# Reordering scaling, transposes and reads inside the states of a selective scan

## The reference, cut to what matters

```python
xi, z = jnp.split(xn @ in_proj, 2, axis=-1)          # 512 channels each
xi = silu(causal_conv4(xi) + conv_b)
dt, Bm, Cm = jnp.split(xi @ x_proj, [16, 32], axis=-1)
delta = softplus(dt @ dt_w + dt_b)
A = -exp(A_log)                                      # 512 channels x 16 states
h = exp(delta * A) * h + (delta * xi) * B            # over the tokens, for each state
y = sum over states of h * C
y = (y + xi * D) * silu(z)
out = x + y @ out_proj
```

## Time and profile before

| | |
|---|---|
| median of 3 runs | 575.18 us (573.67 to 576.09) |
| profiled execution | 575.25 us, of which the traced span is 573.5 us |
| busy: PE, DVE, POOL, ACT | 486.3, 462.5, 387.0, 371.7 us |
| mean granted PE clock | 0.93 of full |

### The profile page before, as it was taken

The page is one execution under the profiler, slowest core; times in us unless marked ns, Lnnn a source line. Parts: engine busy times, 40 slices in busy tenths (PEclk is TensorE's granted clock), DMA queues, the critical chain, the costliest instruction groups (busy, mean ns, idle before and its releaser), DMA issues.

```text
span 573.5 us, 7946 instructions
## 1 busy us (share of the span) xinstructions
PE 486.3 (85%) x2777; PEld 340.7 (59%) x2777; DVE 462.5 (81%) x531; ACT 371.7 (65%) x650; POOL 387.0 (67%) x235
## 2 busy tenths in 40 slices
PE   8968999879868999998689999896797758789992
PEld 6424765455557675655575666465786546678651
DVE  4779989968899888879997888699989989951512
ACT  3766677667875766698858676888558759821210
POOL 5049978756798877759986777589959979510001
PEclk9978999955989999979999999799999979999997
DMA  9331111110111111111111111101211391039004
GB/s 290 107 113 37 38 37 38 39 39 37 34 40 38 37 39 38 39 37 38 38 38 38 38 37 38 39 2 37 75 37 38 110 405 45 2 87 345 0 1 151
DMA packets 17919, 38.88 MB, mean 68 GB/s; under 512 B 1665, under 2 KB 10497, under 8 KB 17874
## 3 DMA queue, kind: packets, MB, share of 16 engines
q1 hardware_dynamic: 17874, 38.32, 19.6%
HBM read 36.08 MB, written 2.23 MB: 67 GB/s over the span
## 4 chain that ended last, share of the span: by engine, by line
PE 47%; DVE 26%; issue 12%; ACT 10%; POOL 2%; DVEq 0%; ACTq 0%; POOLq 0%
DVE scanmem L1724 16%; PE hT L837 9%; PE pp L542 6%; PE pp L566 6%; PE yacc L600 4%; DVE yTd L1744 4%; PE pp L629 4%; PE pp L592 2%; ACT dA L1257 2%; PE dA L802 2%; POOL scanmem L1399 2%; PE pp L578 2%; ACT hc L1267 2%; PE pp L701 1%; PE pp L773 1%
## 5 line engine op out<-in xcount | busy, mean ns | idle before, releaser
L1399 POOL TENSOR_TENSOR scanmem<-par,scanmem 128x1024 f32<-128x1024 f32 x128 | 300.4, 2366 | 87.9 <-ACT carry L1282 41.6
L1257 ACT ACTIVATE dA<-par,Aneg 128x512 f32<-128x512 f32 x256 | 171.1, 690 | 45.2 <-DVE scanmem L1724 43.3
L837 PE MATMUL hT<-con,scanmem 128*128 128x128 f32 x1024 | 153.1, 290 | 43.2 <-DVE yTd L1744 21.3
L837 PEld LDWEIGHTS hT<-con,scanmem 128*128 128x128 f32 x1024 | 121.4, 148 | 100.0 <-issue 35.3
L1724 DVE TENSOR_TENSOR_SCAN scanmem<-dA,scanmem 128x512 f32<-128x512 f32 x128 | 150.3, 1207 | 22.3 <-ACT dA L1257 21.7
L1724 DVE TENSOR_TENSOR_SCAN scanmem<-dA,carry,scanmem 128x512 f32<-128x512 f32 x128 | 157.1, 1267 | 11.8 <-ACT dA L1257 11.5
L1267 ACT ACTIVATE hc<-hT,CTs 128x512 f32<-128x512 f32 x128 | 87.4, 683 | 75.4 <-PE hT L837 75.1
L600 PE MATMUL yacc<-con,hc 128*128 128x128 f32 x512 | 78.8, 294 | 11.2 <-ACT hc L1267 10.9
L600 PEld LDWEIGHTS yacc<-con,hc 128*128 128x128 f32 x512 | 62.9, 151 | 17.6 <-ACT hc L1267 13.7
L1744 DVE SCALAR_TENSOR_TENSOR yTd<-hT,CTs,yTd 128x512 f32<-128x512 f32 x85 | 62.1, 730 | 12.4 <-PE hT L837 12.0
L542 PE MATMUL pp<-xnT,wi 128*128 128x512 f32 x120 | 61.2, 640 | 4.9 <-ACT xnT L1036 3.2
(11 more groups left out here) (195 smaller groups left out, 507.6 us busy)
## 6 DMA issues: line engine op xcount, KB each, us to landing
scanmem<-brow SPq DMA_DIRECT2D x32, 512.0 KB, 3.7
par<-in SPq DMA_DIRECT2D x1, 4096.0 KB, 16.7
scanmem<-in SPq DMA_DIRECT2D x1, 4096.0 KB, 13.9
xt<-in SPq DMA_DIRECT2D x4, 512.0 KB, 6.7
wi<-in SPq DMA_DIRECT2D x2, 1024.0 KB, 7.0
out<-par SPq DMA_DIRECT2D x4, 512.0 KB, 4.1
aw<-in SPq DMA_DIRECT2D x5, 256.0 KB, 6.6
xr<-in SPq DMA_DIRECT2D x1, 1024.0 KB, 9.1
```

What stands on the lines that cost most here:

```text
L837: last = nc.tensor.transpose(hT[:, i % 2, m * P:(m + 1) * P], hb[:, n % RING, m, i * P:(i + 1) * P], ident)
L1257: A(dA[:, m % 2, :], delta(c)[:, m, :], ACT.Exp, scale=Aneg[:, m * NS + s:m * NS + s + 1]).then_inc(da_ready, 1)
L1399: nc.gpsimd.tensor_tensor(hb[:, n % RING, ms, :], dx(c)[:, ms, :], Bb[:, row:row + 1, :].to_broadcast([P, 2, T]), ALU.mult).then_inc(bx_re ...
```

## The change

Nothing is computed differently. Three things move:

1. PE turns block 1 first: T1 (n-1), first jobs, T0 T3 (n-1), R2 (n-2), T2 (n-1), R0 (n-1), second jobs.
2. ACT scales half a state later: M2 (n-2) stands where M0 (n-1) stood, with the carry behind it, and M0 (n-1) where M2 (n-1) stood.
3. DVE reads V and D jobs in the same half as ACT, after the mac, instead of one half later between two scans. The two gates of the even blocks move apart, one to the end of state 0 and one to the end of state 1 of the next chunk; in the last chunk jobs O0, O1 and the first A job go one half later.

```diff
-LAST_EPILOGUE = {1: [("Y", 1)], 2: [("Y", 3)], 3: [("O", 0)], 5: [("O", 1)], 17: [("R", 0)], 19: [("R", 1)]}
-ATT = [6, 8, 8, 10, 12, 14, 15, 16, 17, 20, 22, 23, 24, 27]
+LAST_EPILOGUE = {1: [("Y", 1)], 2: [("Y", 3)], 4: [("O", 0)], 6: [("O", 1)], 17: [("R", 0)], 19: [("R", 1)]}
+ATT = [7, 8, 8, 10, 12, 14, 15, 16, 17, 20, 22, 23, 24, 27]
-LATE = ("V", "D")
+TURNED = (1, 0, 3, 2)
+def turned(n, i):
+    return NT * n + TURNED.index(i) + 1
 # PE, a state
                     if n:
-                        transposes(n - 1, 0)
                         transposes(n - 1, 1)
                     for job in BESIDE[2 * n]:
                         run(job)
                     if n:
+                        transposes(n - 1, 0)
+                        transposes(n - 1, 3)
+                    if n >= 2:
+                        reduce(n - 2, 2)
+                    if n:
                         transposes(n - 1, 2)
-                        transposes(n - 1, 3)
                         reduce(n - 1, 0)
-                        reduce(n - 1, 2)
 # ACT, a state
                     exp_step(n, 0)
                     exp_step(n, 1)
+                    if n >= 2:
+                        mul_step(n - 2, 2)
                     if n:
-                        mul_step(n - 1, 0)
+                        carry_step(n - 1)
                     for job in to_read(2 * n):
                         read(job)
                     exp_step(n, 2)
                     exp_step(n, 3)
                     if n:
-                        mul_step(n - 1, 2)
+                        mul_step(n - 1, 0)
                         pool_mul_step(n - 1)
-                        carry_step(n - 1)
 # DVE, a state
                     scan_step(n, 0)
-                    for job in read_late(2 * n):
-                        read(job)
                     scan_step(n, 1)
                     if n:
                         mac_step(n - 1, 1)
-                    for job in read_by_vector(2 * n):
+                    for job in to_read(2 * n):
                         read(job)
                     scan_step(n, 2)
-                    for job in read_late(2 * n + 1):
-                        read(job)
                     scan_step(n, 3)
                     if n:
                         mac_step(n - 1, 3)
-                    if s == 0 and c:
-                        gate_even(c - 1)
-                    for job in read_by_vector(2 * n + 1):
+                    if s < 2 and c:
+                        gate_even(c - 1, 2 * s)
+                    for job in to_read(2 * n + 1):
                         read(job)
```

More of the change, by code:

```diff
@@ L166, in to_read @@
     return BESIDE[h - 1] if h else []
-def read_by_vector(h):
-    return [job for job in to_read(h) if job[0] not in LATE]
-def read_late(h):
-    return [job for job in to_read(h - 1) if job[0] in LATE] if h else []
 WARM = {**{(name, 1, 0): 2 for name in ("GT", "M", "RR", "PT", "YV", "YT", "VV", "WO")}, ("G", 1, 1): 2,
@@ L822, in transposes @@
             def transposes(n, i):
-                if i == 0:
+                if i == TURNED[0]:
                     pe.wait_ge(scan_done, CT * (n + 1))
@@ L914, in _ @@
             n = NCH * NS
-            for i in range(NT):
-                transposes(n - 1, i)
+            transposes(n - 1, 1)
+            transposes(n - 1, 0)
+            transposes(n - 1, 3)
+            reduce(n - 2, 2)
+            transposes(n - 1, 2)
             reduce(n - 1, 0)
@@ L1262, in mul_step @@
                 e = 2 * n + i // 2
-                act.wait_ge(hT_ready, NT * n + i + 1)
+                act.wait_ge(hT_ready, turned(n, i))
                 if e >= 2:
@@ L1272, in pool_mul_step @@
                 if by_pool(n):
-                    act.wait_ge(hT_ready, NT * n + 4)
+                    act.wait_ge(hT_ready, turned(n, 3))
                     if pool_sums(n) > 2:
@@ L1503, in gate_tile, with gate_even @@
                 return V.tensor_tensor(dx(e)[:, :, t0], o.rearrange("p (m t) -> p m t", m=CT), gate(e)[:, :, t0], ALU.mult)
-            def gate_even(e):
-                for i in (0, 2):
-                    dve.wait_ge(red_done, 2 * (NS * (e + 1) - 1) + i // 2 + 1)
-                    gate_tile(e, i, yacc[:, i // 2, :]).then_inc(gated, 1)
+            def gate_even(e, i):
+                dve.wait_ge(red_done, 2 * (NS * (e + 1) - 1) + i // 2 + 1)
+                gate_tile(e, i, yacc[:, i // 2, :]).then_inc(gated, 1)
             def scale_first(m):
@@ L1730, in mac_step @@
                     return
-                dve.wait_ge(hT_ready, NT * n + i + 1)
+                dve.wait_ge(hT_ready, turned(n, i))
                 dst = yTd[:, c % 2, i // 2, :]
@@ L1771, in _ @@
             mac_step(n - 1, 3)
-            gate_even(NCH - 1)
+            gate_even(NCH - 1, 0)
+            gate_even(NCH - 1, 2)
             for job in BESIDE[-1] + TAIL:
```

## The result

| | before | changed |
|---|---|---|
| median | 575.63 us (573.67 to 576.09, 5 runs) | 559.41 us (558.52 to 567.58, 5 runs) |
| ratio to before | | **0.9735**, 95% interval 0.9694 to 0.9776 |
| profiled execution, span | 575.25, 573.5 us | 562.97, 561.2 us |
| mean granted clock of PE | 0.931 | 0.929 |

A forecast was written before the change was run, and what follows sets the result against it. Bound: PE's work in I and V jobs, a chain of waits in D and Z jobs, then DVE. Entries -2.7, D0 -3.5, Z0 -2.2, late reads +0.3, last chunk -1.5, end +0.3 make -9.3, 575.25 to 566.0 us (range 559.5 to 573).

The forecast's parts named there:

- D0: Job D0, D stretch: its absolute value comes earlier, -1.7 us chunk 1, -1.1 chunk 2, -0.7 chunk 0; sum -3.5.
- Z0: Job Z0, state 12: E2 comes earlier, -1.2 us chunk 1, -0.8 chunk 2, -0.2 chunk 0; sum -2.2.
- Chunk 0's D stretch: Chunk 0, states 9 to 12: PE at half clock and full, so little gain, D0 -0.7 and Z0 -0.2 us.
- Late reads: DVE's D and V reads: moved into a gap where DVE waits anyway, +0.3 us together, bounds -1 and +1.5.
- Entries: Start of each chunk's PE-bound stretch, state 2: I0 starts earlier, -0.7, -1.0 and -1.0 us for chunks 0 to 2.
- Last chunk: Last chunk, states 2 and 3 end 2.2 us earlier, state 4 takes 0.7 back: -1.5 us, bounds +0.5 and -2.5.
- Half clock more often: Rival: T2 waits for ACT every state, PE's clock falls in one more stretch per chunk; 571 us, chance 0.06.
- PE's work takes back the entries: Rival: where PE is full an earlier I0 only lengthens its queue, only D0 and Z0 pay; 570 us, chance 0.18.
- No gain: Rival: earlier D0 only meets scans waiting for something else, chunk times stay within 1 us; 574 us, chance 0.09.
- Slower: Rival: one more turn between M0 and second-half jobs, 0.45 us each, if PE waits for M0; 581 us, chance 0.07.
- inside the stretch: Within the PE-bound stretch of each of three chunks: 0 taken, -0.9 us a chunk kept as far bound.

The follow-up runs named there:

- e2: Changed kernel with VectorE's reads of V and D jobs put back one half later, between two scans: 565.15 us, ratio 0.9821.
- e12: Kernel before with V and D reads in their own half and the last chunk's jobs later, both gates in state 0: 571.32 us.
- e3: Changed kernel with jobs O0, O1 and the first A job of the last chunk at their old halves: 563.33 us.
- e1: Changed kernel with TensorE turning block 0 first again, ScalarE and VectorE as changed: 587.05 us, ratio 1.0198.
- e7: Kernel before with only VectorE's reads of V and D jobs moved to the same half as ScalarE: 572.04 us, ratio 0.9954.
- e4: Kernel before with 16 more matmuls in TensorE's idle time in states 8 and 9 of chunk 0: 573.34 us, ratio 0.9964.
- e5: Changed kernel, unaltered, timed and profiled once more: 563.73 us, ratio 0.9828.
- e6: Changed kernel with 134 more matmuls in TensorE's idle time ahead of first-half jobs, outside the I and V stretches: 564.97 us.
- e10: Kernel before with V and D reads in their own half, gates apart and last chunk's jobs later, old ScalarE and TensorE order: 583.06 us.

## Why the prediction was right, and where it was off

**The order on ScalarE and TensorE is most of the gain, as forecast.** Without the reads (e2) the change is worth 10.4 us by the medians; the forecast for that part was -9.6. Without ScalarE's and TensorE's order, the best that the other parts gave is -4.3 (e12). The two don't overlap much: 10.4 and 3.0 make 13.4 of 13.8. The 10.4 include the last chunk's jobs, 1.5 us by e3, and the moved gate, whose share isn't known. ScalarE's new order alone isn't what pays, since with TensorE's old one it loses (e1), and TensorE's new order alone was not run. That 9.6 and 10.4 lie so close is partly luck: in e2 chunk 0's D stretch gave 4.3 us where 0.9 was forecast, and the last chunk less than its share.

**D0 and Z0 in chunks 1 and 2: the mechanism right, the size partly by luck.** Forecast -2.9 and -1.9, found -2.6 and -3.3 as means. D0 is shown in its rows, and c1 s10 alone went from 10.46 to 8.82 us, -1.6 where -1.7 was forecast. But the reads are in these stretches as well: in e2, the change without them, chunk 1's gave 1.4 us and chunk 2's 3.7, in e7 the reads alone 1.6 and 1.4, and the clocks differ in each.

**Chunk 0's D stretch: the mis-sized term.** "In chunk 0 PE ran at half clock [...] so an earlier ACT has nothing to start: -0.7", and for Z0 -0.2. Found -5.6. The prediction took the half clock of the earlier trace rows as fixed there. It isn't: with 16 matmuls in the wait ahead of it the clock stays up longer and 4.9 us come back (e4). With the change the clock is 0.88, 0.72 and 0.88 in the three profiles, 0.62 before. The reads, too, have a part, 2.1 to 3.7 us alone (e7, e12), so the 5.6 can't be split cleanly.

**Late reads: the wrong step.** "So the move costs nothing and hides the read", +0.3 in the sum, bounds -1 and +1.5. Measured -3.0 alone (e7) and -3.3 as undone (e2), outside the bounds. The prediction's sum of one half looked at how long DVE is busy per half; it left out what the read did at its old place: dA has two buffers, so that a read between S0 and S1 delays the exp after next (e2's rows). State 8 with the last V job's read pays it in full, 7.42 against 6.89 us in chunk 1; the D stretches pay between 0.1 and 1.8 us for four reads.

**Entries: right in size, partly by luck.** -0.7, -1.0, -1.0 forecast; -1.4, -1.1, -1.6 found, of which 0.5 to 0.6 in each chunk is state 8 and belongs to the reads. c1 s2 went from 8.54 to 6.52 us, -2.0 as worked out, and states 3 and 4 gave 1.2 back (6.71 and 8.42 against 5.94 and 7.99), the forecast's size. But only state 3's 0.8 is from T0 and R2 behind I0: state 4 takes 8.42 us in e7 too, where only the reads are moved, and 8.00 in e2. The gate, half a microsecond less in state 0 and as much more in state 1, brought nothing over the two, and at half clock states 0 and 1 of chunk 1 took 15.4 us against 14.4.

**Last chunk: the mechanism right, half of the gain missing.** s2 and s3 went from 14.92 to 12.64, forecast -2.2; s4 took back 1.3, not 0.7; and there was no term for the gate in state 1 and the clock in state 0, which make s0 and s1 up to 0.75 us longer (15.17 in e5, 14.42 before). Behind it, s14 takes 7.0 us in all three profiles instead of 5.4, at clock 0.74 instead of 1.00 (and 5.9 at 1.00 in e6): a fall of the clock that comes with the change and makes about 1.1 of the +1.6 where the prediction had 0; e6's 5.9 has four added matmuls in it. States 8 and 9 gave 1.4 to 1.6 us of it back (7.09 and 11.29 before; 6.7 and 10.05 to 10.3 now), also not forecast.

**The rivals.** "Half clock more often" was the right worry with the wrong sign. The clock of c0 s9-12 is 0.62 with the wait in state 9 and 0.83 with it filled (e4). The Trainium skill, "TensorE: Matmul & The Clock Gate", section "HAM oscillation", says that waits between groups of matmuls put the clock down again and again; by that rule e4's result in chunk 0 is what one expects, and the trace agrees. But the change took waits away as well as adding some, and the mean clock stayed, 0.929 against 0.931, while half clock left much of chunk 0's D stretch and appeared in the last chunk. "PE's work takes back the entries" is excluded by state 2, 2.0 us shorter in chunk 1, of which state 3 takes back 0.8. "No gain" is excluded by every run. "Slower" is excluded by every run; e1 shows that its mechanism is real one turn earlier in the queue, at 25 us.

**The range.** Its low edge isn't the sum of the bounds that it names: -5.5, -3.5 and three times -1.6 with the other terms make -14.7, 560.5 us, and 557.9 with the 0.9 us a chunk inside the stretch. The pooled 13.8 lies in either; the 16.2 of the first medians only in the second.

**What stays open.** Which stretch falls to half clock, and how long it stays down, differs from run to run of the changed kernel (c2 s11, c3 s7, c0 s10), and no run here shows what decides it. The kernel before has one profile only; its runs spread as far (572.3 to 577.4 over all comparisons). With a spread of 5 us, parts worth 1 or 2 us aren't resolved by their medians, and in the D stretches not by one trace each either.

## What to carry to other kernels

Where an in-order engine waits at an instruction whose input is late, let it do the same instruction of one step earlier there; but then move together everything that shares its buffers, since a part moved without its neighbours made the kernel slower than before: the new scaling with the turn of block 0 at its old place (e1), the second gate without the new order (e10). A small read between two links of a double-buffered chain can cost its full length (state 8), even where its engine has idle time over the stretch. And don't write that a stretch "is at half clock, so nothing helps there": the same stretch had a clock of 0.62 to 1.00 in these runs.
